# A transformer layer with eight experts in one kernel: first stacks loaded by halves of heads, weighting and basis functions in another order behind the table, the last block scattered by itself, a constant count and two queues for the final copy

## What is computed

```python
x = x + attn(layernorm(x))      # 16 heads of 8: causal linear attention on a feature map of 2nd order,
                                # and sliding-window softmax attention (window 64); both concatenated @ Wout
x = x + ffn(layernorm(x))

# ffn, for each token: softmax over 8 gate logits, the two largest, weights scaled to sum 1
h       = gelu(x @ mlp_W1[e] + mlp_b1[e]);  mlp_out = h @ mlp_W2[e] + mlp_b2[e]          # experts 0 to 3
basis0  = 1 - tanh((layernorm(x)*g0+b0 - grid) * 0.5)**2      # 8 grid points for each channel
z       = basis0 @ kan_sl_W0[e] + kan_sl_b0[e]                # 1024 -> 256
basis1  = 1 - tanh((layernorm(z)*g1+b1 - grid) * 0.5)**2      # 2048 values
kan_out = basis1 @ kan_sl_W1[e] + kan_sl_b1[e]                # experts 4 to 7
out     = sum over the two chosen experts of weight * expert output
```

## Time and profile before

| | us |
|---|---|
| median of 3 runs | 814.43 |
| lowest and highest run | 813.74, 817.1 |
| the profiled execution, whole | 813.58 |
| its span, first to last instruction | 811.8 |
| TensorE busy | 727.2 (90% of the span) |
| VectorE, ScalarE, GpSimd busy | 474.2, 531.6, 494.7 |

### The profile page before, as it was taken

How to read it: one execution, slowest core, us unless ns; L and a number is a source line. 1 busy time by engine, 2 the same in 40 slices (tenths; PEclk the granted TensorE clock), 3 DMA queues, 4 the chain that set the end, 5 groups by cost and what they waited for, 6 DMA issues and landing times.

```text
span 811.8 us, 20472 instructions
## 1 busy us (share of the span) xinstructions
PE 727.2 (90%) x7113; PEld 556.6 (69%) x7114; DVE 474.2 (58%) x1116; ACT 531.6 (65%) x697; POOL 494.7 (61%) x699
## 2 busy tenths in 40 slices
PE   5499999999999999999989699999999999999860
PEld 2246566575656656566567599989988989899760
DVE  6732655646475554665446594956976949775510
ACT  3577687777767778686783475775876757782700
POOL 9432656465575656657567578668777577656341
PEclk9799999999999999999999799999999999999985
DMA  2530220403114040221361444364463553633124
GB/s 40 160 99 16 72 82 2 142 13 107 48 40 114 3 138 16 85 68 42 91 188 49 97 141 138 69 161 97 131 167 95 127 151 57 164 87 28 14 22 118
DMA packets 72959, 70.61 MB, mean 87 GB/s; under 512 B 20866, under 2 KB 65186, under 8 KB 70948
## 3 DMA queue, kind: packets, MB, share of 16 engines
q1 hardware_dynamic: 55444, 56.88, 22.9%
q0 software_dynamic: 16912, 11.35, 9.8%
q10 hardware_dynamic: 480, 0.79, 0.3%
HBM read 49.43 MB, written 21.37 MB: 87 GB/s over the span
## 4 chain that ended last, share of the span: by engine, by line
PE 69%; DVE 10%; ACT 7%; POOL 5%; issue 4%; DMA 2%; DVEq 0%; ACTq 0%; SPq 0%; POOLq 0%
PE pv L1556 16%; PE ring L1523 13%; PE pv L1643 11%; PE ring L1602 6%; PE ring L1615 4%; PE ring L1490 4%; PE ring L1507 3%; ACT Pb L934 3%; DVE maxima L1192 3%; PE ring L1583 2%; DVE h L1244 2%; PE ring L1705 2%; PE ring L1443 1%; DVE lo L1048 1%; PE ring L1544 1%
## 5 line engine op out<-in xcount | busy, mean ns | idle before, releaser
L934 ACT ACTIVATE Pb<-ring 128x1024 f32<-128x1024 f32 x160 | 156.5, 1025 | 60.8 <-PE ring L1602 58.8
L746 POOL DMA_INDIRECT acc_d<-stack,recs x84 | 138.2, 1645 | 61.7 <-issue 33.3
L767 POOL TENSOR_SCALAR_AFFINE_SELECT Pb<-Pb 128x512 f32<-128x512 f32 x128 | 78.9, 637 | 131.3 <-ACT Pb L934 131.3
L1125 DVE SCALAR_TENSOR_TENSOR stack<-stack 128x512 f32<-128x512 f32 x160 | 103.0, 688 | 59.4 <-ACT stack L912 57.0
L1523 PE MATMUL ring<-stack 128*128 128x256 f32 x560 | 124.0, 381 | 2.5 <-issue 2.3
L1643 PE MATMUL pv<-Pb,vaug 128*32 128x192 f32 (+4 forms) x2048 | 120.4, 376 | 2.3 <-POOL Pb L767 1.6
L1523 PEld LDWEIGHTS ring<-stack 128*128 128x128 f32 x560 | 105.4, 190 | 19.8 <-issue 5.5
L912 ACT ACTIVATE stack<-ring,kprm 128x512 f32<-128x512 f32 x160 | 108.2, 814 | 0.1
L1602 PE MATMUL ring<-stack 128*128 128x128 f16 (+3 forms) x512 | 90.5, 306 | 17.5 <-DMA stack<-hl_d 10.1
L943 ACT ACTIVATE Pb<-ring 128x768 f32<-128x768 f32 (+1 forms) x128 | 88.2, 760 | 15.6 <-PE ring L1615 12.9
L1643 PEld LDWEIGHTS pv<-Pb,vaug 128*32 128x32 f32 x2048 | 60.0, 109 | 55.9 <-issue 37.5
(11 more groups left out here) (237 smaller groups left out, 1148.4 us busy)
## 6 DMA issues: line engine op xcount, KB each, us to landing
stack<-L_ffn_kan_sl_W SPq DMA_DIRECT2D x20, 1024.0 KB, 5.2
stack<-hl_d SPq DMA_DIRECT2D x23, 256.0 KB
stack<-L_ffn_mlp_W SPq DMA_DIRECT2D x12, 256.0 KB
stack<-hl_d SPq DMA_DIRECT2D x23, 128.0 KB
hl_d<-hi SPq DMA_DIRECT2D x7, 384.0 KB, 2.6
hl_d<-lo SPq DMA_DIRECT2D x7, 384.0 KB, 3.3
Pb<-L_ffn_mlp_W SPq DMA_DIRECT2D x10, 256.0 KB, 5.4
xb<-L_attn_x SPq DMA_DIRECT2D x9, 256.0 KB, 2.8
```

The lines of the kernel that those rows point to most:

```text
L746: pool.indirect_dma_start(acc_d, bass.IndirectOffsetOnAxis(ap=recs[:, kind, u % RECS, q, 0:1], axis=0), src[:, u % 2, q, :], None, compute ...
L934: act.activation(Pb[:, n % 2, at:at + 1024].rearrange("p (k q) -> p k q", k=2), slot(job), ACT.Square, bias=1.0).then_inc(freed[job % SLOT ...
L1125: dve.scalar_tensor_tensor(basis[z][g], s_, -1.0, s_, ALU.add, ALU.mult).then_inc(k_bas[z], 1)
```

## The change

Five edits.

1. Batch 0's stacks are loaded by halves of the heads. The first halves (heads 0 to 7, six copies of half the size, and the cleared shift row) count on a new semaphore `first_heads`, for which `begin` of batch 0 now waits; SyncE issues the other halves right behind, ahead of the load of `xb` for batch 1, and the TensorE waits for them ahead of `max` group 1 and `lin` group 2.
2. What prepares `stack[1]` moves. ScalarE's zeros go from behind its stack load to right behind its first instruction; VectorE's two band copies go from ahead of the batches to behind the `max` steps 1 and 3 of group 0 in batch 0; the load of the ones goes to the step `stacks` of batch 0.
3. Behind the table VectorE does statistics, row copy and `weighted(0, 0)` first, and then half of the basis functions of tile 1, `hidden_norm`, the other half, and `load_counts`. The MLP's first weighting operation becomes a plain addition.
4. `kan_second` makes its blocks in the order 3, 2, 1, 0 instead of 3, 2, 0, 1. Block 0 goes to a bank of the ring (`ring[:, 1, 0]`) instead of `pv`, with a signal of its own; VectorE weights blocks 1 to 3 when those are done (`k_three`) and block 0 afterwards, and GpSimd scatters three blocks on the first signal and one on the second. As `hidden_transposed` writes the same bank of the ring, it now waits for `k_y` of the tile before.
5. `all_added` is counted up by each tile's `end_of_add`. SyncE adds, in a loop of 24 turns of its own, one for each tile that there isn't, so that the number waited for is always 49. SyncE and ScalarE each copy one half of the result.

```diff
+        def load_first_heads(eng, s, heads, done):
+            both = 0 if s != 1 else DH
+            hi_again = 2 * DH if s != 1 else 0
+            at, to = (heads.start or 0) * T, (heads.stop or H) * T
+            eng.dma_start(stack[0][s][stack_rows(both, 2 * DH), at:to],
+                          hl_d[s].rearrange("a (d h) t -> (a d) (h t)", d=DH)[:, at:to]).then_inc(done, 16)
...
+            eng.wait_ge(all_added, 2 * TURNS * UNROLL + 1)
+            eng.dma_start(out[B // 2 * m:B // 2 * (m + 1)].rearrange("b t d -> (b t) d"),
+                          acc_d[TS + B * T // 2 * m:TS + B * T // 2 * (m + 1)]).then_inc(copied, 16)
...
             sp.wait_ge(first_stored[2], 32)
             sp.sem_inc(hl_stored, 32)
+            for s in range(3):
+                load_first_heads(sp, s, OTHER_HEADS, stack_loaded[0])
+            sp.sem_inc(stack_loaded[0], 16)
             sp.wait_ge(xres_ready, 1)
...
-            sp.wait_ge(all_added, 1)
-            sp.dma_start(out.rearrange("b t d -> (b t) d"), acc_d[TS:]).then_inc(copied, 16)
-            sp.wait_ge(copied, 16)
+            with sp.Fori(0, TURNS * UNROLL) as k:
+                with sp.If(k >= n_kind[1]):
+                    sp.sem_inc(all_added, 1)
+                with sp.If(k + 1 >= n_kind[0]):
+                    sp.sem_inc(all_added, 1)
+            copy_half(sp, 0)
+            sp.wait_ge(copied, 32)
...
+                    for ready, blocks in ((k_three_y, range(1, Q4)), (k_y, (0,))):
+                        pool.wait_ge(ready, tile_no(k))
+                        pool.sem_inc(pool_at, 1)
+                        for q in blocks:
+                            scatter_block(1, u, q)
...
                 pool.sem_inc(added, 1)
+                pool.sem_inc(all_added, 1)
...
-            load_stack(act, 0, 2)
-            act.activation(stack[1][2][:].bitcast(F32), zeros, ACT.Copy).then_inc(stack1_zeroed, 1)
+            load_first_heads(act, 2, FIRST_HEADS, first_heads)
...
+                        if b == 0 and n == 0 and c in (1, 3):
+                            band_rows(1, c // 2).then_inc(stack1_zeroed, 1)
...
-            n_kind = load_counts(dve)
-            basis_functions(0, 0, 1)
             hidden_stats(0, 0)
             copy_rows(0, 1)
-            weighted(0, 0, 0)
+            weighted(0, 0)
+            basis_functions(0, 0, 1, range(G // 2))
             hidden_norm(0, 0)
+            basis_functions(0, 0, 1, range(G // 2, G))
+
+            n_kind = load_counts(dve)
...
                 pe.wait_ge(k_sig[1], tile_no(k, 2 * G, back=1))
+                pe.wait_ge(k_y, tile_no(k, back=1))
...
-                        mm = pe.matmul(pv[:, 1, P * q:P * (q + 1)], basis[1][g][:, P * q:P * (q + 1)],
+                        mm = pe.matmul(pv[:, 1, P * q:P * (q + 1)] if q else ring[:, 1, 0, 0:P],
+                                       basis[1][g][:, P * q:P * (q + 1)],
...
-                for_blocks(blocks, products, k_mm[1])
+                with pe.If(blocks > 3):
+                    products(3)
+                with pe.If(blocks > 2):
+                    products(2)
+                products(1).then_inc(k_three, 1)
+                products(0).then_inc(k_mm[1], 1)
```

97 lines of the change are left out of this document (62 added, 35 removed).

## The result

The changed kernel takes 824.7 us (median of five runs, 820.4 to 827.0) beside 814.2 for the kernel before: a ratio of 1.0114, with a 95% interval of 1.0092 to 1.0136. A sixth run, a slow one of 1073.5 us at a mean granted clock of 0.652, is left out. The changed kernel is slower by 1.1%, where I had predicted 1.5% faster. Its profiled execution took 822.24 us with a span of 820.2, which stand against 813.58 and 811.8.

The account below looks back on a forecast made before the run. The TensorE, busy 727.2 of 811.8 us, was taken as the bound, with its waits at the start, table and end deciding. 1.0 - 3.5 + 0 - 2.6 - 6.4 - 0.3 = -11.8 gave 802.2 us; eight in ten 798 to 807.

Parts of the forecast that it names:

- The count: At the end: result copy issued at the fourth scatter's landing, skipping GpSimd's 6.65 us through unused tiles; -6.4 us.
- three signs of being wrong: mlp_first still waits over 5 us behind the table, copies start over 5 us after the last scatter, or each turn is longer.
- rival D: Loop: hidden_transposed's new wait for k_y makes the kernel slower than before, 820 if k_y takes 2.8 us; chance 0.04.
- The two queues: At the end: copying the result by two queues saves half of the issue time; -0.3 us, bounds 0 to 3.
- The start: Batch 0's stacks by halves, band copies among the maxima: later `lo` of q and k's projection; +1.0 us, bounds -1.9 to +4.5.
- the walk: At the start: step-by-step timing of VectorE's statistics, reductions and band copies to `lo` of q at 43.6; gave +1.0 us.
- Behind the table: Weighting ahead of the basis functions starts mlp_first and kan_first of tile 1 earlier; -3.5 us, bounds 1.5 to 5.2 saved.
- The low clock: Behind the table: granted clock of 0.50 expected around 454 to 460 us, slowing mlp_first and leaving 3.5 us of gain.
- The loop: Turns over tiles: hidden_transposed's new wait for k_y stays hidden; 0 us, upper bound 4.7.
- it fits narrowly: Loop: weighting block 0, 0.6 to 0.7 us, hides behind the first part of mlp_first, at least 0.87 us.
- The last tile: Blocks 1 to 3 scattered before block 0, held by GpSimd's own landing; -2.6 us, bounds 1.3 to 3.9 saved.

Follow-up runs that it names:

- e1_gate: Changed kernel, but the two result copies wait for one more count, set when GpSimd has left its loop: ratio 1.0107.
- e9_slot: Changed kernel with GpSimd's loop head at a fixed place in its block of instructions: ran once, 918.6 us, no ratio.
- e2_bound: Changed kernel with GpSimd's loop ended by a bound worked out from the count, so it doesn't jump back at the end: ratio 1.0028.
- e10_count_bound: Kernel before with the constant count, GpSimd's and the TensorE's loops ended by a bound from the count, one result copy: ratio 0.9927.
- e3_bands: Changed kernel with VectorE's two band copies back ahead of the batches: ratio 1.0128.
- e6_table: Kernel before with the new order behind the table alone, the weighting keeping its first operation: ratio 0.9958.
- e8_all: Changed kernel with GpSimd's and TensorE's loops bounded, band copies ahead of the batches, block 0 in ring[:, 0], one result copy: ratio 0.9934.
- e4_count: Kernel before with the constant count of all_added alone, and one result copy in SyncE's queue: ratio 1.0059.

## Why the prediction was wrong

**The count, the step that failed.** The prediction said of GpSimd's 6.65 us: "The count now goes up at the landing itself, and SyncE only has to wake". That was right for the copy's issue (-6.5 us). It failed by taking the issue for the end. GpSimd still has to go its way, through the closing barrier, and there it drains for 6.28 us. The trace of before showed the drain, in the instructions of L137: it ended at 803.1 + 6.3 = 809.4, 2.2 us ahead of SyncE's arrival at 811.6. The count does nothing to shorten that chain, so it could never have won more than 2.2 us; the term of -6.4 was impossible. I had gone through the chain of waits and the timeline, neither of which goes beyond the last scatter and the copy. From the copy's issue to the end the runs show +14.9 us in place of the 0 that this term took for granted. None of the prediction's three signs of being wrong came (`mlp_first` waited 1.73 us, the copies started 3.7 us after the last scatter, most turns were as long as before), as none of them concerned the time behind the copy's issue. Of the rivals only D allowed for a slower kernel, by another way, which cost 2.9 us.

**The two queues and the loads.** The term was -0.3; from the issue of the copies to the end it became +14.9. The 23.6 us from the issue to the end are 2.4 of branches for the tiles that there aren't, 9.2 of the load beside the copy, 5.4 of the second and third load, and 6.3 of drain. e1_gate shows the first load without the copy (2.4), e9_slot the other two gone, e2_bound and e10_count_bound the end without all three. The Trainium skill (Runtime: NRT & Kernel Launch, section Instruction fetch mechanics) says that a taken branch out of the two pages at hand forces a DMA fetch of the target page; I had cited it and concluded that the stretch "goes away with the branches". The traces agree with the rule, and the conclusion was wrong, since the branches stay and their fetches now share the DMA engines with the copy. The second queue saved nothing: in the trace of after, the first copy's data begin at 797.9, the second's at 800.9, and both have ended at 805.2, 7.3 us in all, where the one copy before took 6.6. The second landed 11.0 us after its issue, against 8.4.

**The start, mis-sized.** +1.0 was forecast, +3.2 arrived (`lo` of q), of which 2.4 were left at the table. The first `lin` was forecast for 27 and came at 28.87; the stats at 32.28 and the first reduction at 33.48 were about 1.1 us later than forecast, as the rows of batch 1 were issued 4.4 us later behind the six copies. But that is not what made `lo` late: GpSimd began its coefficients only 0.25 us later than before (33.65 and 33.40). The walk priced the band copies on VectorE alone. What they cost is on GpSimd, in the path of `hn`: 1.9 us on the multiplication. The remaining 1.0 us came behind `hn`, where the TensorE ran at a clock of 0.50 after its wait of 3.86 us (q's product took 1.57 us instead of 1.13); the walk had no term for the clock at the start. The selects, 2.0 us longer, come behind `hn` and are not in this path. e3_bands gives 3.7 us back, with the multiplication short and the clock full.

**Behind the table, right.** -3.5 was forecast, -3.2 measured, and e6_table gives 0.4% by itself. The low clock came as expected, though later (0.50 from 458 to 464 us): `mlp_first` ran its first part in 1.99 us and its third and fourth in 3.78.

**The loop, rival D, small in the first trace.** The forecast was 0 with an upper bound of 4.7; it was 2.9, in two turns of ten. In six other traces the loop is longer than before by 3.8 to 11.8 us (see e8_all), so this term was too small as well. The assumption "it fits narrowly" took the time from the last product to `k_y` as two short operations. It is 2.9 us where the tile has two blocks (620.5 to 623.5), as VectorE is still busy with basis functions and `hidden_norm`. The trace of before had the sign: in that turn `k_y` came at 623.2 and the transposes began at 622.0. My argument that VectorE waits for the products was read from a turn with four blocks.

**The last tile, right.** -2.6 forecast, -2.7 measured, with GpSimd held by its own landing until 786.2 as foreseen.

## What to carry to other kernels

A transfer that ends a kernel covers what the other engines still have to do, down to their closing drain. Before it is moved forward, list when each engine reaches the closing barrier: the latest of them is the floor of what can be won. And an engine that has to jump in its code while a large DMA runs can wait for the whole of it; let its loop end before the copy begins, or give it nothing to jump over, and see in the trace that it does arrive: in e8_all the TensorE stood for 6.6 us beside the copy behind a loop that had ended.

A copy on VectorE in an idle time is free only if GpSimd has nothing to do there. A wait that is hidden in the turns of full tiles is to be read again in those of short ones.

## What was unexpected of the hardware

- GpSimd's last drain took 6.28 us in every kernel here.
- GpSimd's jump back to the head of its loop took 2.4 to 3.4 us with no large copy in flight, and 7.5 to 9.2 beside a copy of 2.1 MB, whether in packets of 64 KB or 4 KB. The TensorE's took 5.1 us with no copy (before) and 7.8 and 9.0 beside one (after, e2_bound), but 4.7 where it began 1 us ahead of the copy's data (e4_count).
- Where the head of a loop lies in the code made two more loads of 2.1 to 3.2 us each (gone in e9_slot); one instruction more in each `end_of_add` was enough to bring them (e4_count).
- Beside a VectorE copy of 128x8192 f16, a GpSimd multiplication of 128x4 took 2.91 us instead of 1.02, though it had begun 0.59 us ahead of the copy, and four selects took 4.44 instead of 2.40. The Trainium skill (SBUF — State Buffer, section SBUF: two separate sides) describes an exclusive lock on ports that GpSimd shares with some of VectorE's operations, held by whoever starts first for a whole instruction. The traces agree that one holds the other up; that the first to start keeps the lock does not fit the multiplication, unless its start is placed too early in the profile, where GpSimd's spans are rough.
